# ScalarE takes the last six expert tiles and the last four weight sets; the closing sums move wholly to VectorE

## The chip, the core and the metric

The kernel runs on one core of one Trainium2 chip. Its engines work side by side, each through its own instruction queue: TensorE (PE, matmuls into PSUM), VectorE (DVE), ScalarE (ACT), GpSimd (POOL) and SyncE (SP, which here only issues DMAs). They meet through semaphores. The metric is the device time of one execution, in microseconds, lower is better; the figure shown is the median of three executions.

## The reference, cut to what matters

A small vision tower over 16 images of 256 tokens with 192 features: patch embedding at three scales, attention with 12 heads, and a mixture of 16 experts of which each token uses two. The experts are the part at stake:

```
logits = einsum('bld,ed->ble', x, Wr); probs = softmax(logits)
top_p, top_idx = top_k(probs, 2)                  # gate of token and expert
for each expert e:
    h   = gelu(x @ W1[e] + b1[e])                 # 192 -> 768
    out = h @ W2[e] + b2[e]                       # 768 -> 192
    y  += gate[e] * out
return x + y
```

So the output row of a token is its own row plus gate0 times the output of its first expert plus gate1 times that of its second. There are 16 x 256 x 2 = 8192 (token, expert) pairs.

## The kernel before

**Tiles.** The pairs are sorted by expert into tiles of 128 rows, each tile of one expert. What the router will choose isn't known when the program is built, so it always has the most tiles that can be needed: `NTILE` = 64 + 15 = 79. Tiles 0 to 14 (`NEARLY`) start while attention still runs; 15 to 78 are the stretch that fills the last 330 us. With the given inputs the sixteen experts get 310, 258, 1110, 987, 949, 269, 107, 460, 115, 555, 521, 471, 677, 449, 395 and 559 pairs; each rounded up to whole tiles makes 73. Tiles 0 to 72 hold rows, and 73 to 78 are padding: they are computed all the same, with rows that nobody asks for, and their results go to a part of `pair_rows` that isn't read.

**One tile.** GpSimd fetches its 128 rows from `slot_rows` in device memory into one of four buffers (`t_fetch`, L714). TensorE turns them (`t_rows`, L480, four transposes). VectorE works out where the results go and copies the turned rows out of PSUM (`t_across`, L656 to L661). TensorE multiplies by W1 (`t_up`, L494; both this and the next product run on halves of 64 rows, as two streams). ScalarE adds the bias and applies gelu (`t_gelu`, L530, six instructions). TensorE multiplies by W2 (`t_down`, L506); its two halves leave two partial sums in PSUM. VectorE adds the second bias and the two (`t_biased`, L669 and L670). GpSimd scatters the 128 rows into `pair_rows` (`t_place`, L704). TensorE's order is: up of tile t, turn of tile t+1, down of tile t-1.

**Weights.** SP loads them three tiles ahead into three buffers (`moe_loads`): for each tile two register loads that say which expert and whether it is a new one (L384, L385, `chosen`), two loads of halves of W1 (L392), the biases (L400) and W2 (L406). The loads have a condition: where the expert in the buffer is still the right one, nothing is moved and the semaphore counts on. Each waits until the buffer has been used: W1 of tile t until up of tile t-3, the biases until `m_y` says that the sum of tile t-3 is done, W2 until down of t-3.

**The closing sums.** When its last weight load is issued, SP reads four numbers into registers (L442), which are the counts of scatters that tiles with rows need. It waits for these scatters, not for those of the padding. Then it loads `pair_rows` back in order of tokens: eight chunks, each of two transfers of 384 KB, the first expert's rows into `pair[0]` and the second's into `pair[1]` (L448). ScalarE scales the second by its gate (L545, four instructions each chunk). VectorE multiplies the first by its gate and adds it to the token's row `hr` (L694, four instructions of 128x192), and then adds what ScalarE scaled (L700, one of 128x768). SP stores each chunk to `out` (L452). At the end SP waits for all stores and all 79 scatters.

The order on each engine is written out by hand. VectorE's and ScalarE's closing instructions come behind their last tile, SP's pair loads behind its last weight set.

Of the kernel before, what the change touches and what calls it, by code (L numbers as in the profile page):

```python
# [15 lines left out]
def vit_tower(nc, x0, x1, x2, w0t, w1t, w2t, b012, wft, bf, idx0, idx1, idx2, w_qkv, w_out, b_out, ln_g, ln_b,  # L16
              wrt, ew1, eb1, ew2, eb2, c_ident, c_tri, c_interp1, c_interp2, c_iota, out):
    fp32, bf16, i32, u32 = mybir.dt.float32, mybir.dt.bfloat16, mybir.dt.int32, mybir.dt.uint32
    ALU, ACT, AX = mybir.AluOpType, mybir.ActivationFunctionType, mybir.AxisListType
    ds = bass.ds  # L20

    P = 128
    B, T, E = out.shape
# [26 lines left out]
    NE, _, FF = ew1.shape  # L50
    FC = FF // P
    TOPK = 2
    PAIRS = TOPK * NT
    NTILE = PAIRS + NE - 1

    SEEN = 11
    NEARLY = 15
    assert TOPK * TT * SEEN - (NE - 1) >= NEARLY and NEARLY % 3 == 0
    NREST = NTILE - NEARLY
    NLANE, BY3, SHIFT = NREST // 4, 171, 9  # L60
    assert all(n * BY3 >> SHIFT == n // 3 for n in range(P))
    SEG = P + NT * P
# [22 lines left out]
    with ctx:  # L85
# [222 lines left out]
        def hidden(t):  # L308

            if t < NEARLY:  # L310
# [8 lines left out]
                 "pe_wT act_wT pe_wf act_wf dve_wf dve_g1 dve_b pe_x2T_ act_x2T_ pe_o2 dve_o2 st_o2 ld_x2 ld_o2 pe_x1T_ act_x1T_ pe_o1 act_o1 st_g2 st_g1 ld_g1 st_qA0 st_qA1 st_qB0 st_qB1 ld_qk0 ld_qk1 ld_mx0 ld_mx1 pool_var1 pool_var2 pool_var3 pool_ln pool_h2 pool_r "  # L319
                 "r_dve r_diagd pe_row pe_tot r_tab r_early "  # L320
                 "m_x0 m_x1 m_x2 m_x3 m_wa0 m_wa1 m_wa2 m_wb0 m_wb1 m_wb2 m_f0 m_f1 m_f2 m_f3 m_tr m_xT m_s1 m_gelu m_s2 m_y "
                 "m_sc0 m_sc1 m_sc2 m_sc3 ld_p0 ld_p1 ld_p2 ld_p3 ld_p4 ld_p5 ld_p6 ld_p7 c_first c_out c_gated "
                 "out_done dve_lane st_bias m_b0 m_b1 m_b2 r_hot").split()
        s = {n: sem(n) for n in names}

# [38 lines left out]
        def wait_prev(eng, which, count):  # L364

            if not (isinstance(count, int) and count <= 0):
                eng.wait_ge(which, count)


        def moe_loads(sp):  # L370
# [53 lines left out]
            second(1, *two)  # L424
            second(2, *three)
            before = None
            for t in range(NW, NTILE):
                if t == NEARLY:
                    biases(t - 1, *before)
                    second(t - 1, *before)  # L430
                    sp.wait_ge(s["r_tab"], 1)
                now = chosen(t)
                first(t, *now)
                if NW < t != NEARLY:
                    biases(t - 1, *before)
                    second(t - 1, *before)
                before = now
            biases(NTILE - 1, *before)
            second(NTILE - 1, *before)

            sp.wait_ge(s["r_hot"], 1)
            counts = [sp.value_load(r_tr[2][0:1, m:m + 1], min_val=16 * (PAIRS // NB), max_val=16 * (NTILE // NB + 1))  # L442
# [56 lines left out]
        def t_down(pe, t):  # L499
            p, w = t % 2, t % NW  # L500
            pe.wait_ge(s["m_gelu"], 2 if t == 0 else t + 1)
            pe.wait_ge(s[f"m_wb{w}"], 16 * (t // NW) + 16)
            wait_prev(pe, s["m_y"], t)
            for c in range(FC):
                for h, rows in enumerate((LO, HI)):
                    last = nc.tensor.matmul(Y[h], hT[p][rows, c * P:(c + 1) * P], w2b[w][rows, c, :],  # L506
                                            start=(c == 0), stop=(c == FC - 1))
            last.then_inc(s["m_s2"], 1)
# [14 lines left out]
        def t_gelu(act, t):  # L523
            p = t % 2
            w = t % NW
            act.wait_ge(s[f"m_b{w}"], 16 * (t // NW) + 16)
            act.wait_ge(s["m_s1"], t + 1)
            wait_prev(act, s["m_s2"], t - 1)
            for c in range(FC):
                last = nc.scalar.activation(hT[p][:, c * P:(c + 1) * P], hidden(t)[c], ACT.Gelu, bias=bias[w][:, c:c + 1])  # L530
            last.then_inc(s["m_gelu"], 1)

        def moe_scalar(act):
            for t in range(NEARLY, NTILE):
                t_gelu(act, t)
                if t == NEARLY + NREST // 2:
                    act.wait_ge(s["dve_ls"], B)
                    own = ex[:, NT - DEFER * TT:NT, :]
                    nc.scalar.activation(own, own, ACT.Exp).then_inc(s["act_ex"], 1)
                    nc.scalar.activation(warm[:, :], epsc[:, 0:1], ACT.Gelu)  # L540
            act.wait_ge(s["r_hot"], 2)
            for c in range(NC):
                act.wait_ge(s[f"ld_p{c}"], 32)
                for t in range(CT):
                    last = nc.scalar.activation(pair[1][c][:, t, :], pair[1][c][:, t, :], ACT.Copy,  # L545
                                                scale=r_gate[1][:, c * CT + t:c * CT + t + 1])
                last.then_inc(s["c_gated"], 1)

        done = [0]

# [120 lines left out]

        def moe_vector(dve):
            V = nc.vector
            for t in range(NEARLY - 2, NTILE):
                t_biased(dve, t)
                if t + 3 < NTILE:
                    t_across(dve, t + 3)
                if t == NEARLY + 4:
                    then(dve, V.tensor_scalar(r_tr[0][:, :], iota[:, 0:NB], ends[:, NE - 1:NE], float(NEARLY), ALU.add, ALU.add))
                    then(dve, V.tensor_scalar(r_tr[1][:, :], r_tr[0][:, :], 2, None, ALU.arith_shift_right))  # L680
                    then(dve, V.tensor_copy(r_trf[:, :], r_tr[1][:, :]))
                    V.tensor_scalar(r_tr[2][:, :], r_trf[:, :], 16.0, None, ALU.mult).then_inc(s["r_hot"], 1)
                if t == NEARLY + NREST // 2 + 2:
                    dve.wait_ge(s["act_ex"], B - DEFER + 1)
                    then(dve, V.tensor_reduce(r_sum[:, :], ex[:, :, 0:NE], AX.X, ALU.add))
                if t == NEARLY + NREST // 2 + 3:
                    then(dve, V.reciprocal(r_gate[0], r_sum[:, :]))
                    V.tensor_tensor(r_gate[1], ex[:, :, NE + 1], r_gate[0], ALU.mult).then_inc(s["r_hot"], 1)

            dve.wait_ge(s["pool_r"], B)  # L690
            for c in range(NC):
                dve.wait_ge(s[f"ld_p{c}"], 32)
                for t in range(c * CT, (c + 1) * CT):
                    last = V.scalar_tensor_tensor(hr[:, t, :], pair[0][c][:, t - c * CT, :], r_gate[0][:, t:t + 1],  # L694
                                                  hr[:, t, :], ALU.mult, ALU.add)
                last.then_inc(s["c_first"], 1)
                h = hr[:, c * CT:(c + 1) * CT, :]
                dve.wait_ge(s["c_gated"], c + 1)
                dve.wait_ge(s["c_first"], c + 1)
                V.tensor_tensor(h, h, pair[1][c], ALU.add).then_inc(s["c_out"], 1)  # L700

        def t_place(pool, t):
            pool.wait_ge(s["m_y"], t + 1)
# [1343 lines left out]
```

## Time and profile before

| | us |
|---|---|
| three executions | 808.65, 810.04, 814.27 |
| median | 810.04 |
| profiled execution, first to last instruction (span) | 776.9 |
| TensorE busy in it | 693.9 (89%) |
| VectorE busy | 459.1 (59%) |
| ScalarE busy | 372.5 (48%) |
| GpSimd busy | 389.3 (50%) |
| DMA queue of SP, share of 16 engines | 39.6% |

The own device time of the profiled execution isn't listed beside its span. The median of the three timed executions lies 33.1 us above that span (starting and ending the program). Busy shares are means over the whole span; what matters here is its last 50 us, which the rows below show.

In rows of a timeline or a chain the first number is the start in us from the beginning of the span, the second the time in us that the piece took. What stands in brackets behind a row is how long the engine had been idle and what ended that.

### The profile page before, as it was taken

What the parts mean: (1) busy time and instruction counts of PE and PEld (TensorE: products, weight loads), DVE (VectorE), ACT (ScalarE), POOL (GpSimd) and SP (SyncE); (2) the same over time, 40 slices, a digit from 0 to 9 for tenths busy, and PEclk for the clock granted to TensorE, in tenths of its full rate; (3) what the DMA queues carried; (4) which work ended last, traced back from release to release, by engine and by line L of the source; (5) the groups of instructions that cost most, each with busy time, mean ns of one, the idle gap of its engine ahead of it and who ended that gap; (6) DMA issues with size and microseconds to landing.
All of it is one profiled execution on the core that took longest, in us unless ns stands there. A gap on an engine that the chain in (4) does not pass through costs nothing.

```text
span 776.9 us, 22765 instructions
## 1 busy us (share of the span) xinstructions
PE 693.9 (89%) x7879; PEld 598.0 (77%) x7879; DVE 459.1 (59%) x1322; ACT 372.5 (48%) x892; POOL 389.3 (50%) x599
## 2 busy tenths in 40 slices
PE   0597689999999999999889999999999999999970
PEld 0486557777677777777657999999999999999970
DVE  7301345788888888888876764444444444443448
ACT  0232246666666666666565433334434453443443
POOL 6772123557777777777666553333433343343320
PEclk9999769999999999999999999999999999999995
DMA  8776624434444444444429634748348325498159
GB/s 208 140 114 190 140 60 108 112 89 121 103 110 103 111 115 114 109 109 111 108 66 264 189 106 121 220 141 227 91 128 236 97 76 149 123 288 240 50 182 331
DMA packets 96795, 110.69 MB, mean 142 GB/s; under 512 B 18625, under 2 KB 85186, under 8 KB 96386
## 3 DMA queue, kind: packets, MB, share of 16 engines
q1 hardware_dynamic: 79202, 79.56, 39.6%
q0 software_dynamic: 11792, 27.18, 11.7%
q10 hardware_dynamic: 5712, 2.79, 2.0%
q8 instruction: 52, 0.85, 0.5%
q14 instruction: 37, 0.30, 0.1%
HBM read 142.13 MB, written 33.96 MB: 227 GB/s over the span
## 4 chain that ended last, share of the span: by engine, by line
PE 57%; DVE 12%; issue 9%; POOL 8%; DMA 5%; SPq 4%; ACT 1%; POOLq 1%; DVEq 0%; ACTq 0%
PE BK L506 20%; PE BK L494 20%; PE BK L828 4%; PE BK L962 3%; PE BK L921 2%; POOL slot_rows L1896 2%; POOL rs L1845 2%; PE BK L941 2%; DVE negmax L1567 2%; DMA level_patches<-pixels 2%; POOL hr L1885 1%; DVE hr L694 1%; PE BK L973 1%; DMA level_rows<-shared 1%; SPq L746 1%
## 5 line engine op out<-in xcount | busy, mean ns | idle before, releaser
L530 ACT ACTIVATE pixels<-BK,shared 128x128 f32<-128x128 f32 x474 | 130.7, 375 | 197.1 <-PE BK L494 166.0
L494 PE MATMUL BK<-pixels,shared 64*128 64x128 f32 x2844 | 172.8, 272 | 2.0 <-issue 2.0
L506 PE MATMUL BK<-shared,pixels 64*128 64x192 f32 x1896 | 172.4, 328 | 2.3 <-DVE pixels L670 2.2
L704 POOL DMA_INDIRECT pair_rows<-pixels x79 | 77.9, 985 | 190.4 <-DVE pixels L670 183.9
L494 PEld LDWEIGHTS BK<-pixels,shared 64*128 64x128 f32 x2844 | 169.1, 188 | 3.3 <-issue 3.1
L506 PEld LDWEIGHTS BK<-shared,pixels 64*128 64x128 f32 x1896 | 153.3, 188 | 4.3 <-issue 3.9
L1567 DVE TENSOR_REDUCE negmax<-BK 128x6 f32<-128x1536 f32 x64 | 112.4, 1757 | 27.9 <-PE BK L941 26.6
L1317 ACT ACTIVATE shared<-BK 128x1536 f32<-128x1536 f32 x64 | 92.7, 1448 | 9.5 <-PE BK L962 9.1
L1896 POOL DMA_INDIRECT slot_rows<-xr,adr x64 | 64.7, 1011 | 36.8 <-issue 13.8
L669 DVE TENSOR_TENSOR pixels<-BK,shared 128x192 f32<-128x192 f32 x79 | 28.2, 357 | 71.1 <-PE BK L506 70.8
L656 DVE TENSOR_TENSOR pixels<-pixels 128x1 int32<-128x1 f32 x64 | 10.2, 159 | 89.9 <-PE BK L480 89.9
L941 PE MATMUL BK<-shared 96*128 96x256 bf16 x384 | 56.0, 284 | 4.5 <-DMA shared<-qk_parts 4.0
L962 PE MATMUL BK<-shared 99*128 99x256 bf16 x384 | 54.0, 278 | 0.7 <-ACT shared L1317 0.6
L1851 POOL TENSOR_TENSOR shared<-shared 128x512 bf16<-128x512 f32 (+1 forms) x32 | 29.1, 909 | 49.6 <-ACT shared L1298 48.9
L973 PE MATMUL BK<-shared,v 128*32 128x256 f32 x768 | 51.2, 385 | 1.0 <-ACT oT L1323 1.0
L941 PEld LDWEIGHTS BK<-shared 96*128 96x128 bf16 x384 | 36.0, 101 | 16.5 <-DMA shared<-qk_parts 4.4
L962 PEld LDWEIGHTS BK<-shared 99*128 99x128 bf16 x384 | 35.8, 99 | 12.3 <-ACT shared L1317 3.9
L714 POOL DMA_DIRECT2D pixels<-slot_rows x64 | 37.0, 578 | 4.2 <-issue 4.1
L1829 POOL DMA_INDIRECT pixels<-x,i x32 | 33.4, 1043 | 9.7 <-issue 9.7
L1323 ACT ACTIVATE oT<-BK 128x256 f32<-128x256 f32 x48 | 18.3, 381 | 39.0 <-PE BK L973 38.9
L1845 POOL TENSOR_TENSOR rs<-var,mhalf 128x2 f32<-128x2 f32 x48 | 34.0, 709 | 3.8
L973 PEld LDWEIGHTS BK<-shared,v 128*32 128x32 f32 x768 | 20.2, 109 | 17.3 <-issue 3.4
(239 smaller groups left out, 1073.6 us busy)
## 6 DMA issues: line engine op xcount, KB each, us to landing
shared<-ew SPq DMA_DIRECT2D x158, 288.0 KB
shared<-ew SPq DMA_DIRECT2D x79, 576.0 KB
shared<-qk_parts SPq DMA_DIRECT2D x112, 96.0 KB
shared<-expert_biases SPq DMA_DIRECT2D x79, 99.0 KB
pixels<-slot_rows POOLq DMA_DIRECT2D x64, 104.0 KB
qk_parts<-shared SPq DMA_DIRECT2D x32, 192.0 KB, 2.0
shared<-qk_parts SPq DMA_DIRECT2D x16, 288.0 KB
shared<-pair_rows SPq DMA_DIRECT2D x12, 384.0 KB, 7.6
```

What stands on the lines that cost most here:

```text
L494: last = nc.tensor.matmul(hidden(t)[h * HC + c], w1h[w][rows, (k + h) % NK, c * P:(c + 1) * P], xtT[p][rows, k, :], start=(c == 0 and k == ...
L506: last = nc.tensor.matmul(Y[h], hT[p][rows, c * P:(c + 1) * P], w2b[w][rows, c, :], start=(c == 0), stop=(c == FC - 1))
L530: last = nc.scalar.activation(hT[p][:, c * P:(c + 1) * P], hidden(t)[c], ACT.Gelu, bias=bias[w][:, c:c + 1])
L704: nc.gpsimd.indirect_dma_start(pair_d, bass.IndirectOffsetOnAxis(t_dst[:, t:t + 1], 0), ysum[t % NB][:, :], None).then_inc(s[f"m_sc{t % NB ...
L714: nc.gpsimd.dma_start(xt[t % NB][:, :], slot_d[ds(at, P), :]).then_inc(s[f"m_f{t % NB}"], 16)
L941: last = nc.tensor.matmul(S[:, a, t * T:(t + 1) * T], qs[p][0:KS, h, t * P:(t + 1) * P], ks[p][0:KS, h, :], start=True, stop=True)
L962: last = nc.tensor.matmul(dst[:, a, t * T:(t + 1) * T], ks[p][:, h, t * P:(t + 1) * P], qs[p][:, h, :], start=True, stop=True)
L973: last = nc.tensor.matmul(dst[32 * a:32 * a + 32, 0:T], v[p][:, t, GU * g + a, :], pT[:, GU * g + a, t * T:(t + 1) * T], start=(t == 0), s ...
L1317: nc.scalar.activation(pT[:, HU * u:HU * u + HU, :], src[:, :, :], ACT.Exp).then_inc(s["act_exp"], 1)
L1567: nc.vector.tensor_reduce(negmax[:, :, HU * u:HU * u + HU].rearrange("p t h -> p h t"), S[:, :, :].rearrange("p a (t k) -> p a t k", t=TT) ...
L1845: nc.gpsimd.tensor_tensor(rs[:, :], var[:, :], mhalf[:, :], ALU.pow).then_inc(done, 1)
L1896: nc.gpsimd.indirect_dma_start(slot_d, bass.IndirectOffsetOnAxis(adr[p][:, k, t:t + 1], 0), xr[p][:, t, k, :], None).then_inc(s[f"st_id{p} ...
```

## The change

`LATE` is 79 - 6 = 73 and `AHEAD` is 2.

- **SP** issues weight sets up to tile 74 instead of 78. Its register loads, waits and pair loads follow directly.
- **ScalarE** issues the weight sets of tiles 75 to 78 (`late_weights`), with the same register loads, waits and conditions. It also turns over the rows of tiles 75 to 78 (`late_across`: four instructions in place of VectorE's four) and copies the result of tiles 73 to 78 out of PSUM (`late_copied`). It no longer scales anything in the closing sums.
- **TensorE**: in tiles 73 to 78 down isn't split in halves: one matmul of the identity with the replicated second bias starts the sum, and six of 128 rows follow, all into one PSUM area, so that only a copy is left to do.
- **VectorE** stops after the sum of tile 72 and the turned rows of tile 74. Its closing sums have four instructions with the first gate and four with the second for each chunk.

```diff
+    LATE = NTILE - 3 * NE // 8
+    AHEAD = 2
 ...
-            for t in range(NW, NTILE):
+            for t in range(NW, LATE + AHEAD):
 ...
-            biases(NTILE - 1, *before)
-            second(NTILE - 1, *before)
+            biases(LATE + AHEAD - 1, *before)
+            second(LATE + AHEAD - 1, *before)
 ...
         # t_down
+            if t >= LATE:
+                nc.tensor.matmul(Y[0], ident[:, :], bias[w][:, FC:FC + E], start=True, stop=False)
+                for c in range(FC):
+                    last = nc.tensor.matmul(Y[0], hT[p][:, c * P:(c + 1) * P], w2b[w][:, c, :],
+                                            start=False, stop=(c == FC - 1))
+                last.then_inc(s["m_s2"], 1)
+                return
 ...
+        def late_across(act, t):
+            p = t % 2
+            act.wait_ge(s["m_tr"], t + 1)
+            nc.scalar.activation(t_dst[:, t:t + 1], xt[t % NB][:, E:E + 1], ACT.Identity, bias=offm[:, t:t + 1])
+            act.wait_ge(s["m_s1"], t - 1)
+            nc.scalar.activation(xtT[p][:, 0:2, :]..., XT[:, :, :, :]..., ACT.Copy)
+            nc.scalar.activation(xtT[p][LO, 2, :]..., XT[HI, :, 1, :], ACT.Copy)
+            nc.scalar.activation(xtT[p][HI, 2, :]..., XT[LO, :, 0, :], ACT.Copy).then_inc(s["m_xT"], 1)
+
+        def late_copied(act, t):
+            r = t % NB
+            act.wait_ge(s["m_s2"], t + 1)
+            act.wait_ge(s[f"m_sc{r}"], 16 * (t // NB))
+            nc.scalar.activation(ysum[r][:, :], Y[0], ACT.Copy).then_inc(s["m_y"], 1)
+
+        def late_weights(act, t):
+            w = t % NW
+            e = act.value_load(tab[0:1, t:t + 1], min_val=0, max_val=NE - 1)
+            new = act.value_load(r_new[0:1, t:t + 1], min_val=0, max_val=1)
+            act.wait_ge(s["m_s1"], t - NW + 1)
+            for h in range(2):
+                nc.scalar.dma_start(w1h[w][h * RT:(h + 1) * RT, :, :], ew1[...], cond=new) \
+                    .then_inc(s[f"m_wa{w}"], 16)
+            act.wait_ge(s["m_y"], t - NW + 1)
+            nc.scalar.dma_start(bias[w][:, :], bias_d[...], cond=new).then_inc(s[f"m_b{w}"], 16)
+            act.wait_ge(s["m_s2"], t - NW + 1)
+            nc.scalar.dma_start(w2b[w][:, :, :], ew2[...], cond=new).then_inc(s[f"m_wb{w}"], 16)
+
         def moe_scalar(act):
             for t in range(NEARLY, NTILE):
+                if t + 1 >= LATE + AHEAD and t + 1 < NTILE:
+                    late_across(act, t + 1)
                 t_gelu(act, t)
+                if t > LATE:
+                    late_copied(act, t - 1)
+                if LATE <= t < NTILE - AHEAD:
+                    late_weights(act, t + AHEAD)
 ...
-            act.wait_ge(s["r_hot"], 2)
-            for c in range(NC):
-                act.wait_ge(s[f"ld_p{c}"], 32)
-                for t in range(CT):
-                    last = nc.scalar.activation(pair[1][c][:, t, :], pair[1][c][:, t, :], ACT.Copy,
-                                                scale=r_gate[1][:, c * CT + t:c * CT + t + 1])
-                last.then_inc(s["c_gated"], 1)
+            late_copied(act, NTILE - 1)
 ...
         # moe_vector
-            for t in range(NEARLY - 2, NTILE):
+            for t in range(NEARLY - 2, LATE):
                 t_biased(dve, t)
-                if t + 3 < NTILE:
+                if t + 3 < LATE + AHEAD:
                     t_across(dve, t + 3)
 ...
             for c in range(NC):
                 dve.wait_ge(s[f"ld_p{c}"], 32)
-                for t in range(c * CT, (c + 1) * CT):
+                at = range(c * CT, (c + 1) * CT)
+                for t in at:
                     last = V.scalar_tensor_tensor(hr[:, t, :], pair[0][c][:, t - c * CT, :], r_gate[0][:, t:t + 1],
                                                   hr[:, t, :], ALU.mult, ALU.add)
                 last.then_inc(s["c_first"], 1)
-                h = hr[:, c * CT:(c + 1) * CT, :]
-                dve.wait_ge(s["c_gated"], c + 1)
                 dve.wait_ge(s["c_first"], c + 1)
-                V.tensor_tensor(h, h, pair[1][c], ALU.add).then_inc(s["c_out"], 1)
+                for t in at:
+                    last = V.scalar_tensor_tensor(hr[:, t, :], pair[1][c][:, t - c * CT, :], r_gate[1][:, t:t + 1],
+                                                  hr[:, t, :], ALU.mult, ALU.add)
+                last.then_inc(s["c_out"], 1)
```

How the instructions stand now is seen at two places. First VectorE at its last tile and its first closing chunk. `pixels` is the memory of the tiles' buffers, `BK` is PSUM, `shared` holds weights and the loaded pairs. Before (the last two sums, of tiles 77 and 78, have nothing between them):

```order
L661 COPY pixels<-BK 64x128
L669 TENSOR_TENSOR pixels<-BK,shared 128x192
L670 TENSOR_TENSOR pixels<-BK,pixels 128x192
L694 SCALAR_TENSOR_TENSOR hr<-shared,r_gates,hr 128x192 x4
L700 TENSOR_TENSOR hr<-hr,shared 128x768
```

and with the change, where the sum of tile 72 is the last:

```order
L705 COPY pixels<-BK 64x128
L713 TENSOR_TENSOR pixels<-BK,shared 128x192
L714 TENSOR_TENSOR pixels<-BK,pixels 128x192
L740 SCALAR_TENSOR_TENSOR hr<-shared,r_gates,hr 128x192 x4
L745 SCALAR_TENSOR_TENSOR hr<-shared,r_gates,hr 128x192 x4
```

The sums of tiles 73 to 78 and the copies of tiles 75 to 78 have left VectorE, and a chunk is eight instructions of 128x192 instead of four and one of 128x768.

Second ScalarE. Before, its last tiles are six gelu instructions each and nothing between them, then the scaling of the first chunks:

```order
L530 ACTIVATE pixels<-BK,shared 128x128 x186
L545 ACTIVATE shared<-shared,r_gates 128x192 x16
L545 ACTIVATE v<-v,r_gates 128x192 x8
L545 ACTIVATE xr<-xr,r_gates 128x192 x8
```

and with the change one of its tiles (75), from the turned rows of tile 76 to the weight set of tile 77:

```order
L545 ACTIVATE pixels<-pixels 128x1
L547 ACTIVATE pixels<-BK 128x256
L549 ACTIVATE pixels<-BK 64x128
L550 ACTIVATE pixels<-BK 64x128
L539 ACTIVATE pixels<-BK,shared 128x128 x6
L557 ACTIVATE pixels<-BK 128x192
L561 TENSOR_LOAD pixels
L562 TENSOR_LOAD pixels
L565 DMA shared<-ew 64x3x384
L570 DMA shared<-expert_biases 128x198
L573 DMA shared<-ew 128x6x192
```

Between two gelus of ScalarE now stand five more instructions, two register loads (with the register operations behind each, left out here as the second of the two W1 halves is) and four DMA issues.

## Rows read from the trace of the kernel before

**Rows 1.** The page's part 4: the chain that ended last, by engine

```profile
PE 57%; DVE 12%; issue 9%; POOL 8%; DMA 5%; SPq 4%; ACT 1%; POOLq 1%; DVEq 0%; ACTq 0%
```

**Rows 2.** By stretch: PE, PEld, DVE, ACT, POOL busy us, granted clock, DMA share, GB/s

```profile
720.00:730.00 10.00, 10.00 (x154) 10.00 (x152) 4.64 (x16) 4.97 (x18) 3.74 (x6) 1.00 0.19 59
```

**Rows 3.** The chain that ended last, in order of time: start, us, what

```profile
754.72 1.42 DVE hr L694 x4
...
756.23 0.96 DVE hr L700
757.19 1.33 DVE hr L694 x4
...
772.88 0.96 DVE hr L700
```

**Rows 4.** Timeline around tile 72: start, us, engine, line, operation

```profile
727.47 0.08 SPq L406 DMA_DIRECT2D shared<-ew  x1
...
730.80 0.36 DVE L670 TENSOR_TENSOR pixels<-BK,pixels 128x192 f32<-128x192 f32 x1
...
731.44 0.99 POOL L704 DMA_INDIRECT pair_rows<-pixels  x1 [2.31 <-DVE pixels L670]
...
732.47 1.66 ACT L530 ACTIVATE pixels<-BK,shared 128x128 f32<-128x128 f32 x6 [2.48 <-PE BK L494]
```

**Rows 5.** Timeline: SP's last weight loads, its first pair loads, its stores

```profile
737.26 0.54 SPq L392 DMA_DIRECT2D shared<-ew  x2
...
743.98 0.07 SPq L406 DMA_DIRECT2D shared<-ew  x1
...
746.63 4.28 SPq L448 DMA_DIRECT2D shared<-pair_rows  x9
...
757.21 17.03 SPq L452 DMA_DIRECT2D out<-hr  x8
```

**Rows 6.** Timeline: ScalarE as chunks 1, 2 and 8 land; GpSimd's last scatter

```profile
750.95 1.49 ACT L545 ACTIVATE shared<-shared,r_gates 128x192 f32<-128x192 f32 x4 [0.30 <-DMA shared<-pair_rows]
...
754.08 1.49 ACT L545 ACTIVATE shared<-shared,r_gates 128x192 f32<-128x192 f32 x4 [1.64 <-DMA shared<-pair_rows]
...
755.08 0.96 POOL L704 DMA_INDIRECT pair_rows<-pixels  x1 [2.19 <-DVE pixels L670]
...
766.74 1.49 ACT L545 ACTIVATE xr<-xr,r_gates 128x192 f32<-128x192 f32 x4 [0.45 <-DMA xr<-pair_rows]
```

**Rows 7.** DMA view 731.5 to 735.5, GB/s in 40 slices of 0.1 us

```profile
GB/s 0 0 0 0 0 0 0 0 0 0 0 0 0 0 0 553 184 154 93 0 0 0 291 455 166 175 50 25 0 0 0 0 0 0 0 0 42 0 0 0
```

**Rows 8.** DMA view 730 to 746: all packets, GpSimd's queue, SP's conditional W2 loads

```profile
DMA packets 279, 0.60 MB, mean 37 GB/s; under 512 B 96, under 2 KB 160, under 8 KB 276
...
q0 software_dynamic: 276, 0.56, 10.6%
...
shared<-ew SPq DMA_DIRECT2D x4, 576.0 KB
```

**Rows 9.** DMA view 774 to 777, the last store alone, 40 slices of 0.075 us

```profile
GB/s 0 0 0 0 0 0 0 0 0 0 113 297 348 328 297 328 328 328 328 328 328 328 317 328 328 328 226 41 0 0 0 0 0 0 0 0 0 0 0 0
DMA packets 528, 0.39 MB, mean 131 GB/s; under 512 B 16, under 2 KB 528, under 8 KB 528
```

**Rows 10.** DMA view 760 to 761, packets of GpSimd's queue

```profile
q0 software_dynamic: 8, 0.01, 3.3%
```

**Rows 11.** SP's pair loads, from issue to landing

```profile
DMA to landing us min/median/max: 3.3/8.9/12.2
```

**Rows 12.** TensorE by shape: down's halves, and full-row products (busy, mean ns)

```profile
L506 PE MATMUL BK<-shared,pixels 64*128 64x192 f32 x1896 | 172.4, 328 | 2.3 <-DVE pixels L670 2.2
...
L893 PE MATMUL BK<-lng_b,ident 128*128 128x192 f32 x56 | 11.8, 356 | 2.8 <-DMA pixels<-level_rows 2.8
...
L873 PE MATMUL BK<-w2f,shared 128*128 128x192 f32 x24 | 4.2, 330 | 0.0
```

**Rows 13.** ScalarE by line: a PSUM copy of 128x256

```profile
L1323 ACT ACTIVATE oT<-BK 128x256 f32<-128x256 f32 x48 | 18.3, 381 | 39.0 <-PE BK L973 38.9
```

More of the change, by code:

```diff
@@ L321, in vit_tower @@
                  "m_x0 m_x1 m_x2 m_x3 m_wa0 m_wa1 m_wa2 m_wb0 m_wb1 m_wb2 m_f0 m_f1 m_f2 m_f3 m_tr m_xT m_s1 m_gelu m_s2 m_y "
-                 "m_sc0 m_sc1 m_sc2 m_sc3 ld_p0 ld_p1 ld_p2 ld_p3 ld_p4 ld_p5 ld_p6 ld_p7 c_first c_out c_gated "
+                 "m_sc0 m_sc1 m_sc2 m_sc3 ld_p0 ld_p1 ld_p2 ld_p3 ld_p4 ld_p5 ld_p6 ld_p7 c_first c_out "
                  "out_done dve_lane st_bias m_b0 m_b1 m_b2 r_hot").split()
@@ L531, in t_gelu @@
             last.then_inc(s["m_gelu"], 1)
+        def late_across(act, t):
[3 more added lines that the diff above has]
+            act.wait_ge(s["m_s1"], t - 1)
+            nc.scalar.activation(xtT[p][:, 0:2, :].rearrange("p s (h t) -> p s h t", h=2),
+                                 XT[:, :, :, :].rearrange("p h s t -> p s h t"), ACT.Copy)
+            nc.scalar.activation(xtT[p][LO, 2, :].rearrange("p (h t) -> p h t", h=2), XT[HI, :, 1, :], ACT.Copy)
+            nc.scalar.activation(xtT[p][HI, 2, :].rearrange("p (h t) -> p h t", h=2), XT[LO, :, 0, :], ACT.Copy) \
+                .then_inc(s["m_xT"], 1)
@@ new lines, in late_copied @@
+        def late_copied(act, t):
[9 more added lines that the diff above has]
+            for h in range(2):
+                nc.scalar.dma_start(w1h[w][h * RT:(h + 1) * RT, :, :],
+                                    ew1[ds(e, 1), :, h * (FF // 2):(h + 1) * (FF // 2)].rearrange("a (k r) f -> r (a k) f", r=RT),
+                                    cond=new) \
+                    .then_inc(s[f"m_wa{w}"], 16)
+            act.wait_ge(s["m_y"], t - NW + 1)
+            nc.scalar.dma_start(bias[w][:, :], bias_d[ds(e, 1), :, :].rearrange("a p n -> p (a n)"), cond=new) \
+                .then_inc(s[f"m_b{w}"], 16)
+            act.wait_ge(s["m_s2"], t - NW + 1)
+            nc.scalar.dma_start(w2b[w][:, :, :], ew2[ds(e, 1), :, :].rearrange("a (c p) d -> p (a c) d", p=P),
+                                cond=new) \
+                .then_inc(s[f"m_wb{w}"], 16)
@@ L690, in moe_vector @@
             dve.wait_ge(s["pool_r"], B)
+            dve.wait_ge(s["r_hot"], 2)
             for c in range(NC):
                 dve.wait_ge(s[f"ld_p{c}"], 32)
-                for t in range(c * CT, (c + 1) * CT):
+                at = range(c * CT, (c + 1) * CT)
+                for t in at:
                     last = V.scalar_tensor_tensor(hr[:, t, :], pair[0][c][:, t - c * CT, :], r_gate[0][:, t:t + 1],
```

## The prediction

> **What bounds the kernel now.** I looked first at where the chain of waits ends. Over the whole span it is TensorE's, 57% [rows 1]; by stretches TensorE is busy all of 720 to 730 at full clock [rows 2], and only its own work can shorten that. The change touches nothing of it before tile 73. So the question is the tail. There the chain goes over to VectorE, to the closing sums, and stays on it to the end: the first chunk starts at 754.72 and the last instruction ends at 772.88 + 0.96 = 773.84 [rows 3]. The span ends at 776.9, 3.06 later: one store (its last packets pass at 774 + 28 x 0.075 = 776.1) and its semaphore [rows 9].
>
> A tile takes 1.66 + 2.48 = 4.14 us (ScalarE's work and its idle time between two gelus) [rows 4]. The sum of tile 72 ends at 731.16, its scatter is issued at 731.44 [rows 4]. SP's first pair load is issued at 746.63 [rows 5], 15 us later, though tile 72 is the last with rows. What held SP is its queue: the last weight load is issued at 743.98, and behind it are only four register loads, (746.63 - 744.05) / 4 = 0.65 us each [rows 5]. No time is left there for a wait on scatters. VectorE was held too: chunk 1 is in memory at 750.95 [rows 6], and its sum starts at 754.72, behind tile 78.
>
> **The change, part by part.**
>
> *SP is let go earlier.* Its last weight load, of tile 74, is issued at 727.47 [rows 4]; the register loads end at 727.55 + 2.58 = 730.1. Now a real wait comes last: tile 72's scatter. Its data pass from 733.0, the burst ending at about 733.4 (the second burst is GpSimd's fetch) [rows 7]. For the semaphore I add 0.6, between 0 and the 0.8 by which the last store's packets precede the end of the span [rows 9]. Pair loads from 734.0 (733.4 to 734.4), 12.6 earlier than 746.63.
>
> *The chunks land* as they did, counted from the first load: chunk 1 after 4.3, chunk 2 after 7.45, chunk 8 after 20.1 (ScalarE's starts in [rows 6] minus 746.63, where it had been idle for DMA): at 738.3, 741.45 and 754.1. Stores don't delay them in either kernel, since SP issues all sixteen loads first.
>
> *VectorE's chunk grows.* Before it is 1.33 + 0.09 + 0.96 = 2.38 (757.19 to 759.57) [rows 3]. The 0.96 becomes four instructions, 1.42 from a standing start [rows 3], so a chunk is 1.33 + 0.09 + 1.42 = 2.84. Chunk 1 ends at 741.2, before chunk 2 is there; from then on VectorE is the slower side: 741.45 + 7 x 2.84 = 761.3. That is 8 x 0.46 = 3.7 us of the gain given back, and ScalarE's scaling (1.49 per chunk [rows 6]) was no cost before, being hidden. With the last store 761.3 + 3.1 = **764.4**.
>
> *The stores as a floor.* They follow the loads in SP's queue. A lone one takes 17 slices of 0.075, 1.3 us [rows 9]; eight behind 754.1 make 764.5, and with the 0.8 behind the last packets 765.3 as an upper value, less where several are under way.
>
> *ScalarE's late tiles.* Before, it rests 2.48 of 4.14 us per tile [rows 4]. Added are: turned rows, one of 128x256 out of PSUM 0.38 [rows 13], two of 64x128 and one of 128x1 at no more than a gelu instruction each (1.66 / 6 = 0.28), 1.2 in all; the result 0.4 (between 1.49 / 4 and the 0.44 that a lone one may take) [rows 6]; a weight set, two register loads 1.3, the W1 pair 0.54, W2 0.07 [rows 5], biases with their register work about 0.4, together 2.3 to 2.4. Tiles 74, 75 and 76 cost 1.66 + 1.2 + 0.4 + 2.4 = 5.7 us, more than TensorE's period: ScalarE sets the pace there. Followed step by step from gelu 73 (up 73 ends near 728.2, as gelu 73 used to start at 728.3): ScalarE is free at 729.8, at 732.2 with weight set 75, at 738.1 with set 76, at 743.8 with set 77, at 749.5 with set 78. So up 77 starts at 745.1 and up 78 at 750.8, about 1 us of stall each, up 78 some 4 later than before. The last result is copied at 758.3, where VectorE's last ended at 754.4 before.
>
> *TensorE's unsplit down.* 24 half instructions become 14 full ones (each matmul of 32-bit data shows as two). Full-row products of the same width took 4.2 / 24 = 0.175 and 11.8 / 56 = 0.21 each [rows 12]: 2.45 to 2.95 per tile, against 172.4 / 79 = 2.18 [rows 12]. I take 2.5, as the cheaper row has the same kind of operands; partly hidden by ScalarE, the dearer end adds 1.0, 759.3.
>
> *The last scatter.* Issued 0.3 behind the result. With SP's queue full, a scatter issued at 755.08 still had packets between 760 and 761 [rows 6, 10], 5.9 later; in the quiet stretch it took 2.0 (731.44 to 733.4). So it ends between 758.6 + 2.0 and 759.6 + 5.9, plus 0.8: 761.4 to 766.3, beside the other ends and not behind them. SP waits for it last.
>
> *Conditional loads on ScalarE's queue.* Set t + 2 is now issued after gelu t: set 76 at about 737.5, needed at 739.4. In 730 to 746, where SP issues four whole sets that move nothing, there are 279 packets, 276 of them GpSimd's, and 0.60 MB [rows 8]. A transfer that moves data leaves 16 packets under 512 B beside its data (528 with them) [rows 9]; a skipped one leaves none. So I take its completion as 0 to 2 us, which costs nothing to 0.2. The Trainium skill (DMA: Bandwidth & Descriptors, Why a DMA increments its semaphore by 16 and not by 1) has the completion as each engine's last descriptor, a write that lands only after that engine's data. By it a skipped load would stand in line with the pair loads; that is rival 3.
>
> *Nothing else*: the row fetch of tile 78 is issued before the pair loads, no table load is added, and the tiles ahead of 73 are unchanged.
>
> **Sum.** Three ends stand at 764.4, up to 765.3, and 761.4 to 766.3. I take **765**: 776.9 - 765 = 11.9 us less. The profiled execution is known by its span alone; the median of 810.04 lies 33.1 above it, and I let that stand: 765 + 33.1 = **798**. Less than 1% (8.1 us, 801.9 to 818.1) can't be told from no change.
>
> **The rivals.**
>
> 1. *ScalarE and TensorE become the bound.* If a weight set costs 3 on ScalarE, full-row products 2.95 and each stall another 0.3, the last result comes 3 to 4 later, near 762, and with 0.3 + 5.9 + 0.8 the span ends at 769: 802. For it: ScalarE has no rest in three tiles. Against: only four sets move.
>
> 2. *VectorE and GpSimd block each other.* A sum now runs beside six scatters instead of one. If VectorE stood still for each (0.96 us), 6 x 0.96 = 5.8 us: 770, 803. The trace speaks against it: the sums from 754.72 take 1.42 beside the scatter of 755.08 [rows 3, 6], no more than elsewhere (1.33 on the chain behind others). The Trainium skill (SBUF — State Buffer, SBUF: two separate sides) says that a VectorE instruction with two SBUF inputs and a GpSimd instruction that reads SBUF take one port pair in turn, each for its whole length; by that the same price.
>
> 3. *Slower: skipped loads land like loaded ones.* If the semaphores of sets 76 to 78 come L after the issue, tile 76's up waits, and set 78, issued later for it, makes tile 78's wait again, so beyond about 3 us each us of L costs 2. With L = 8.9, the median of pair loads [rows 11], the last result is at 770.4, the span ends near 774, 807. With 12.2, their longest [rows 11], at 777.0, plus 0.3 + 2.0 + 0.8 = 780.1: 813, slower than before. It decides from L = 10.6, where 773.8 + 3.1 = 776.9. Against: the missing packets [rows 8].
>
> 4. *It doesn't do what it says.* If SP's counts included padding, its wait would move to tile 78's scatter, and 30.3 us (746.63 to 776.9) would follow 761: 791, 824. But SP started its loads at 746.63, before tile 76 was scattered, and without any wait.
>
> **How the numbers follow.** Forecast 0.62; rival 1, 0.17; rival 2, 0.05; rival 3, 0.07; rival 4, 0.02; below 794 (chunks landing sooner in a quiet queue) 0.03; something unseen, slower, 0.04. The range: 761.4 + 33.1 = 794 is the low end (all ends at their early values, and no tail behind VectorE's 761.3); up to 805 it takes in rivals 1 and 2; left out are rivals 3 and 4 and the unseen, about 0.16. Faster by over 1%: the forecast, the early case and three quarters of rival 1, 0.78. Within 1%: the rest of rival 1, rival 2, most of rival 3, 0.17. Slower: 0.05.
>
> **What would show it.** Right: SP's first pair load near 734; VectorE's first closing instruction near 738, its last ending near 761, eight chunks 2.84 apart without DMA waits after the second; idle time of TensorE of about 1 us ahead of up 77 and up 78; ScalarE's last copy near 758 and the last scatter near 765. Wrong: ScalarE's late period above 6 us, up 76 waiting for weights (rival 3), sums above 0.35 us apart while scatters are issued (rival 2), or a first pair load after 740 (rival 4).

## The result: 795.85 us, and the profile after

| | before | after |
|---|---|---|
| median of the runs, us | 809.35 (808.18 to 814.27, 4 runs) | 795.85 (794.4 to 801.02, 4 runs) |
| ratio, 95% interval | | 0.9843 (0.98 to 0.9886) |
| span of the profiled execution | 776.9 | 795.1 |
| from the end of tile 72's sum to the end of the span | 45.7 | 33.1 |

The kernel is 13.5 us faster, by the ratio 9 to 16 us. The forecast was 798. That the span of the trace after is longer than that of the first trace of before, with a shorter device time, is taken up below: the first trace lacks a stretch of idle time at the start which every later trace but one (pads_first) has. So the two are compared from the end of tile 72's sum on: 731.16 before (730.80 + 0.36) [rows 4], 761.96 after. From here on "+x" is x us behind that sum.

The timeline after, around tile 72 and the first chunks (start, us, engine, line, operation; in brackets the idle time ahead of it and what ended it):

```profile
761.60 0.36 DVE L714 TENSOR_TENSOR pixels<-BK,pixels 128x192 f32<-128x192 f32 x1
...
762.24 0.99 POOL L751 DMA_INDIRECT pair_rows<-pixels  x1 [2.31 <-DVE pixels L714]
...
764.99 5.74 SPq L450 DMA_DIRECT2D shared<-pair_rows  x9
...
769.84 1.40 DVE L740 SCALAR_TENSOR_TENSOR hr<-shared,r_gates,hr 128x192 f32<-128x192 f32 x4 [7.88 <-DMA shared<-pair_rows]
...
771.27 1.41 DVE L745 SCALAR_TENSOR_TENSOR hr<-shared,r_gates,hr 128x192 f32<-128x192 f32 x4
...
772.66 1.40 DVE L740 SCALAR_TENSOR_TENSOR hr<-shared,r_gates,hr 128x192 f32<-128x192 f32 x4
```

SP's first pair load is at +3.03, where it was at +15.5 [rows 5], and VectorE's first closing sum at +7.9, where it was at +23.6 (754.72) [rows 3]. VectorE has one wait left, for the first chunk. SP's longest is for a scatter; its other long ones, of up to 3.5 us, are between the stores, for VectorE's sums. The waits of SP after, from 760 on (who waited for whom, us in total, times, longest):

```profile
SPq L454 <- DVE hr L745: 9.7, 6, 3.5
SPq L447 <- DMA pair_rows<-pixels: 4.1, 1, 4.1
SPq L87 <- DMA out<-hr: 1.9, 1, 1.9
```

L447 is the wait for the scatters of tiles with rows; before it did not show, as its engine came to it late. The chain of what waited last (start, us, what) now runs over that scatter and the first chunk's load, to VectorE's sum at 769.84:

```profile
762.24 2.67 DMA pair_rows<-pixels
...
765.39 4.31 DMA shared<-pair_rows
```

L458, at the very end, is the wait for the scatters of all 79 tiles, and the 1.9 us of L87 behind it are the wait for the last store. The end of the chain after (start, us, what) answers to [rows 3]:

```profile
785.14 1.41 DVE hr L745 x4
786.55 1.33 DVE hr L740 x4
...
787.90 1.41 DVE hr L745 x4
789.31 1.33 DVE hr L740 x4
...
790.66 0.42 DVE hr L745
791.08 0.33 DVEq L87
791.41 0.66 DVE hr L745 x2
```

A chunk is 1.41 + 1.35 = 2.76 (785.14 to 787.90; the 1.35 is the 1.33 and 0.02 before the next), without waits, and VectorE ends at 791.41 + 0.66 = 792.07, +30.1; the span ends 3.03 later.

ScalarE and TensorE after, from up 76 to up 77: the copy of tile 74's result, weight set 77, down 75, gelu 76; and the last copy and the last scatter:

```profile
770.49 2.28 PE L496 MATMUL BK<-pixels,shared 64*128 64x128 f32 x36
...
771.10 0.37 ACT L557 ACTIVATE pixels<-BK 128x192 f32<-128x192 f32 x1
...
771.95 0.53 ACTq L565 DMA_DIRECT2D shared<-ew  x2
...
772.82 0.59 PE L507 MATMUL BK<-shared,ident 128*128 128x192 f32 x2
...
773.25 2.11 PE L509 MATMUL BK<-shared,pixels 128*128 128x192 f32 x12
...
774.43 1.67 ACT L539 ACTIVATE pixels<-BK,shared 128x128 f32<-128x128 f32 x6
...
775.29 2.28 PE L496 MATMUL BK<-pixels,shared 64*128 64x128 f32 x36
...
787.90 0.33 ACT L557 ACTIVATE pixels<-BK 128x192 f32<-128x192 f32 x1 [2.69 <-PE BK L509]
788.51 0.97 POOL L751 DMA_INDIRECT pair_rows<-pixels  x1 [2.06 <-ACT pixels L557]
```

The late period (from one tile's first product to the next one's) is 775.29 - 770.49 = 4.80, and TensorE fills it. Before the change it was 4.13 (742.57 to 746.70). The unsplit down accounts for 2.54 - 2.20 = 0.34 of the difference if its length alone is counted; no run asked where the rest comes from. The last result is copied at 788.23, +26.3.

### The profile page after: what moved, and what is told of

It reads as the page before. It is cut to its first block, busy times and chain, and to the rows that moved or that the text cites. A ratio compares the mean times of both kernels' runs of the same rounds, so it can differ in the third digit from the quotient of the medians.

```text
span 795.1 us, 22622 instructions
## 1 busy us (share of the span) xinstructions
PE 699.7 (88%) x7819; PEld 601.2 (76%) x7819; DVE 454.0 (57%) x1318; ACT 367.9 (46%) x882; POOL 387.7 (49%) x599
## 4 chain that ended last, share of the span: by engine, by line
issue 38%; PE 18%; POOL 16%; DVE 13%; another core or an unknown queue 5%; POOLq 4%; DMA 3%; ACT 2%; SPq 1%; DVEq 0%; ACTq 0%
POOL pixels L761 5%; PE BK L875 4%; POOL slot_rows L1943 3%; PE BK L1009 3%; POOLq L760 3%; PE BK L968 2%; POOL pair_rows L751 2%; POOL rs L1892 2%; DVE negmax L1614 2%; PE BK L988 2%; PE BK L1020 2%; POOL hr L1932 2%; DVE hr L745 1%; DVE hr L740 1%
## 5 line engine op out<-in xcount | busy, mean ns | idle before, releaser
L496 PE MATMUL BK<-pixels,shared 64*128 64x128 f32 x2844 | 175.1, 273 | 1.8 <-issue 1.7
L515 PE MATMUL BK<-shared,pixels 64*128 64x192 f32 x1752 | 160.0, 328 | 3.0 <-DVE pixels L714 1.6
L515 PEld LDWEIGHTS BK<-shared,pixels 64*128 64x128 f32 x1752 | 142.3, 187 | 4.7 <-issue 3.9
L713 DVE TENSOR_TENSOR pixels<-BK,shared 128x192 f32<-128x192 f32 x73 | 26.1, 357 | 42.8 <-PE BK L515 39.8
L1890 POOL TENSOR_TENSOR var<-mv,epsc 128x2 f32<-128x2 f32 x48 | 9.3, 194 | 73.3 <-DVE mv L1579 73.2
L1370 ACT ACTIVATE oT<-BK 128x256 f32<-128x256 f32 x48 | 18.4, 383 | 40.5 <-PE BK L1020 40.5
L1892 POOL TENSOR_TENSOR rs<-var,mhalf 128x2 f32<-128x2 f32 x48 | 34.1, 710 | 3.8
L1876 POOL DMA_INDIRECT pixels<-x,i x32 | 30.7, 961 | 9.7 <-issue 9.7
```

Source lines behind the costliest of these rows:

```text
L496: last = nc.tensor.matmul(hidden(t)[h * HC + c], w1h[w][rows, (k + h) % NK, c * P:(c + 1) * P], xtT[p][rows, k, :], start=(c == 0 and k == ...
L1892: nc.gpsimd.tensor_tensor(rs[:, :], var[:, :], mhalf[:, :], ALU.pow).then_inc(done, 1)
```

## The experiments

All times are ratios to runs of the kernel before on the same chip. The tail is read from each trace as above, from the end of tile 72's sum to the end of the span; it is not touched by what varies earlier (that sum ends anywhere between 760 and 766 in the traces). Each tail is one trace's.

| run | ratio, 95% interval | first pair load | first sum | tail |
|---|---|---|---|---|
| before, second trace | 0.9993 (0.9959 to 1.0027) | +15.5 | +23.55 | 45.8 |
| SP alone let go | 1.0006 (0.9978 to 1.0033) | +2.7 | +23.56 | 45.8 |
| VectorE alone let go | 1.0026 (1.0001 to 1.0051) | +17.35 | +21.8 | 47.1 |
| both gates on VectorE, nothing else | 1.0058 (1.0023 to 1.0093) | +15.5 | +23.56 | 48.8 |
| change, scaling left on ScalarE | 1.0026 (1.0002 to 1.005) | +3.3 | +7.9 | 48.3 |
| change, late W2 products twice | 0.9957 (0.9933 to 0.9981) | +3.2 | +8.0 | 42.0 |
| change, ScalarE scales three chunks | 0.9821 (0.9788 to 0.9855) | +2.9 | +8.2 | 33.2 |
| change, second trace | 0.9804 (0.9767 to 0.9842) | +2.9 | +8.7 | 33.9 |

**The kernel before again (base_again).** No edit.

> The kernel before, unchanged, for a second trace. Theory A: the 33.1 us that I put outside the span of the first trace are a stretch inside, at the start (the changed kernel's trace has TensorE, VectorE and ScalarE idle from about 34 to 64 us, and only 1.7 us outside its span). Then the span is about 807, 1.7 below the device time, with that idle stretch in it, and from the sum of tile 72 to the end it is 45.7 us as in the first trace. Rival: the idle stretch came with the change; then the span is about 777 and has no such stretch. Time 809, ratio 1.00 by both.

Span 811.4 with a tail of 45.8 (about 807 was expected; that execution took 813.71). The stretch is there. By stretch (PE, PEld, DVE, ACT, POOL busy us, clock, DMA share, GB/s), first in the first trace of before, then in this one:

```profile
40.00:60.00 20.00, 18.25 (x127) 15.66 (x125) 0.56 (x1) 7.20 (x10) 15.43 (x18) 1.00 0.78 121
```

```profile
40.00:60.00 20.00, 0.00 (x0) 0.00 (x0) 0.00 (x0) 0.00 (x0) 13.70 (x16) 1.00 0.26 49
```

Its waits of 20 to 90 us:

```profile
ACT w2f L1252 <- remote: 39.5, 1, 39.5
PE BK L828 <- ACT b1T L1256: 31.9, 1, 31.9
DVE hbias L1510 <- remote: 26.7, 1, 26.7
```

From about 34 to 64 GpSimd is the only one of the four computing engines that works; SP issues loads until about 41. Theory A holds: outside the span lie 1.7 us (796.82 against 795.1 in the profiled execution after), and about 30 of the 33.1 that I put outside are this stretch. It was there in the changed kernel as well, so it cancels between the two. No execution of the kernel before on record came below 806.49, though its first trace spans only 776.9: the first trace is the odd one. "Remote" says that the profile doesn't know who released the two engines.

**SP alone (sp_alone).** The kernel before, with `late_weights` in ScalarE's loop and SP's loop ending at tile 74:

```diff
-            for t in range(NW, NTILE):
+            for t in range(NW, LATE + AHEAD):
 ...
                 t_gelu(act, t)
+                if LATE <= t < NTILE - AHEAD:
+                    late_weights(act, t + AHEAD)
```

> The kernel before, with the last four weight sets issued by ScalarE, so that SP goes on to the pair loads; VectorE keeps all its tiles and ScalarE the scaling. Theory (both must be let go): pair loads start 3 us after the sum of tile 72 instead of 15.5, but VectorE begins its closing sums behind tile 78 as before, 23.5 us after the sum of tile 72; the tail from that sum to the end stays 45.7 us (45.3 to 46.5), time 809. Rival (SP's queue is what held the tail): 12.4 us less, 33 us, time 797.

The sum of tile 72 ends at 764.52 here. Pair loads at +2.7, VectorE's first sum at +23.56, tail 45.8:

```profile
767.24 5.67 SPq L450 DMA_DIRECT2D shared<-pair_rows  x9
...
788.08 1.41 DVE L716 SCALAR_TENSOR_TENSOR hr<-shared,r_gates,hr 128x192 f32<-128x192 f32 x4
```

12.8 us earlier loads bring nothing. The rival falls.

**VectorE alone (dve_alone).** The changed kernel, SP's loop to `NTILE` again, `late_weights` not called.

```diff
-            for t in range(NW, LATE + AHEAD):
+            for t in range(NW, NTILE):
 ...
-                if LATE <= t < NTILE - AHEAD:
-                    late_weights(act, t + AHEAD)
```

> The changed kernel, but SP issues all 79 weight sets as before; ScalarE has the late tiles, VectorE is free from tile 73 on and does both gates. Theory (both must be let go): SP's last set waits for the sum of tile 75, 14.4 us behind that of tile 72 at the slower late period of 4.8, so the first pair load comes at 17.5; plus 7.45 for chunk 2, 7 x 2.78 for the sums and 3.05 for the last store is a tail of 47.5 us, 1.8 more than before: 811. Rival (VectorE's release is what gives it): a tail near 33, 797.

VectorE stands idle for the first chunk:

```profile
788.13 1.41 DVE L738 SCALAR_TENSOR_TENSOR hr<-shared,r_gates,hr 128x192 f32<-128x192 f32 x4 [21.80 <-DMA shared<-pair_rows]
```

The tail is 47.1, 1.3 us longer than before (1.8 expected). Each half of the change alone is worth nothing or less, both together 12.6 us in the first trace's tail and 11.9 in the second's: whichever engine is still held sets the start of the sums.

**Both gates on VectorE (sums_alone).** The kernel before with the changed closing sums.

```diff
-                h = hr[:, c * CT:(c + 1) * CT, :]
-                dve.wait_ge(s["c_gated"], c + 1)
-                V.tensor_tensor(h, h, pair[1][c], ALU.add).then_inc(s["c_out"], 1)
+                for t in at:
+                    last = V.scalar_tensor_tensor(hr[:, t, :], pair[1][c][:, t - c * CT, :], r_gate[1][:, t:t + 1],
+                                                  hr[:, t, :], ALU.mult, ALU.add)
+                last.then_inc(s["c_out"], 1)
```

> The kernel before, but VectorE adds both gated halves of a chunk itself (eight instructions of 128x192) and ScalarE scales nothing. Theory: VectorE is the bound of the closing stretch from 23.5 us after the sum of tile 72 on, and a chunk costs 2.78 instead of 2.38, so 8 x 0.4 = 3.2 us more: tail 48.9, time 812.5. Rival (the wait for ScalarE was part of the chunk, or transfers bound it): no difference, 45.7 and 809.

Tail 48.8, 3.0 us more: this is what the change pays back, 8 x 0.38.

**The scaling left on ScalarE (scal_keeps).** The changed kernel with the old closing loop on both engines, ScalarE's behind its last copy.

```diff
             late_copied(act, NTILE - 1)
+            act.wait_ge(s["r_hot"], 2)
+            for c in range(NC):
+                act.wait_ge(s[f"ld_p{c}"], 32)
+                ... (four instructions with scale, c_gated)
```

> The changed kernel, but ScalarE scales the second half of each chunk as before the change, behind its last copy, and VectorE adds 128x768. Theory (the scaling had to leave ScalarE, since its queue now ends 26.3 us behind the sum of tile 72): chunk 1 can be finished only at 27.8, then 2.38 each, tail 27.8 + 0.96 + 7 x 2.38 + 3.06 = 48.5 us against 33.1, time near 811 to 813. Rival (a chunk of 2.38 instead of 2.76 wins, ScalarE is idle enough): tail 30 to 33, time at or below the changed kernel.

VectorE starts at +7.9 and then waits 18.4 us for ScalarE (its one wait for L596, the scaling); tail 48.3 (48.5 expected). Left behind ScalarE's last tile, the scaling costs the whole gain and more. Where ScalarE has no weight set left to issue there is room for some of it, as scal_helps below shows.

**The late products twice (down_twice).** In padding tiles the W2 products are added a second time, into rows that nobody reads.

```diff
-                for c in range(FC):
+                for c in range(2 * FC):
+                    c, end = c % FC, c == 2 * FC - 1
```

> The changed kernel, with the six W2 products of each padding tile done twice (their results are not read, the output is unchanged). It asks how far TensorE's late tiles are from the bound. A late period of 4.8 becomes 6.9, so the last copy moves from 26.3 to 38.9 us behind the sum of tile 72, and the last scatter with its wait follows some 3 to 6 later. Theory: TensorE's side takes over, tail 42 to 45 us against 33.1, time near 806; VectorE's sums end where they did, 30 us behind that sum. Rival (the end waits for the stores alone): 33.1.

Its late tiles take 6.75 (from copy to copy; 6.9 expected), and the last result is copied at +38.0 (38.9 expected). Its waits of SP:

```profile
SPq L458 <- DMA pair_rows<-pixels: 9.5, 1, 9.5
SPq L454 <- DVE hr L746: 8.2, 4, 3.3
SPq L447 <- DMA pair_rows<-pixels: 4.2, 1, 4.2
```

L458 is the last wait for scatters; it was 0.2 us in the changed kernel and is 9.5 here. VectorE's last sum ends at +30.7, half a microsecond later than it did. So the mechanism of rival 1 of the prediction is real, but it needs more: 11.7 us of added time on TensorE's side (last copy at +38.0 instead of +26.3) made the tail 8.9 longer. By this, TensorE's side had 2.8 us of slack. In the changed kernel itself SP came out of the wait for the last scatter 1.9 us before the last store landed, and that scatter's packets passed until 792.4, 3.9 us behind its issue at 788.51, beside stores; in down_twice, with the stores done, they took 2.3 (799.24 to 801.5). So the slack is 2 to 3 us, and part of it appears only because a later scatter passes sooner.

**ScalarE scales three chunks (scal_helps).** Chunks 5, 7 and 8, behind the results of tiles 76, 77 and 78, so that VectorE has 128x768 there.

```diff
+        SCALED = {77: (4,), 78: (6,), 79: (7,)}
 ...
+                for c in SCALED.get(t, ()):
+                    scaled(act, c)
```

> The changed kernel, but ScalarE scales chunks 5, 7 and 8 in gaps of its late tiles (behind the results of tiles 76, 77 and 78). Theory (VectorE's eight chunks are the bound from 7.9 us behind the sum of tile 72 to 3 us before the end): three chunks are 0.4 shorter, tail 31.9 to 32.2 instead of 33.1; the last scatter, whose packets end some 2 us before the last store's, is the next bound. Rival (stores or scatter bound it already): 33.1 again. Over the whole 0.1%, less than the timed runs can tell; the tail in the trace decides.

VectorE's eight chunks took 21.5 (772.23 to 793.70) instead of 22.2, though it also waited 0.55 for chunk 2. It began 0.35 us later than in the changed kernel, so its last sum is at +29.7, 0.4 earlier. The tail is 33.2 all the same, as the rival had it; the 31.9 to 32.2 of the theory did not come. SP's queue is full at 789 to 790 (first row: packets, MB, share of 16 engines) and still at 795 to 796 (second row):

```profile
q1 hardware_dynamic: 503, 0.37, 110.5%
```

```profile
q1 hardware_dynamic: 387, 0.28, 91.5%
```

In the changed kernel the traffic had run down to 20 to 30 GB/s from 792.4 to 792.9, before its last store. The span ends 3.5 us behind VectorE's last sum, where it was 3.03. So of the 0.75 us that VectorE's stretch became shorter, 0.35 went into the later start and 0.47 into stores still in line. With one trace this shows that VectorE and the stores end close to each other, and no gain that the timed runs could tell.

**The changed kernel again (after_again).** No edit.

> The changed kernel, unchanged, for a second trace and a narrower time. Theory: tail from the sum of tile 72 to the end 33.1 us (32.8 to 33.6), so 12.6 us less than before, time 0.984 to 0.985 of before; the idle stretch from 34 to 64 us is there as in the kernel before. Rival (part of the measured 13.5 us is chance in the start stage): the ratio is nearer to 0.99, with the same tail.

Tail 33.9, 11.9 us less than the second trace of before; 32.8 to 33.6 was expected. The 33.1 of the first trace was the short end. The three kernels below have the same closing stretch, and their tails are 34.1, 33.5 and 34.3. In all five traces the tail is 25.3 to 25.5 behind VectorE's first sum (+7.9, +8.7, +8.8, +8.2, +8.8), so what varies is when the first chunk lands.

The whole is 0.9804 (0.9767 to 0.9842), where 0.984 to 0.985 was expected: faster by 12.8 to 19 us. What it has beyond the tail, 0 to 7 us, no trace explains; the end of tile 72's sum differs by as much from trace to trace.

**The stall at the start (pads_first, pads_mid, pads_8th).** The changed kernel, with GpSimd's two stores of padding rows ahead of its 32 gathers, behind 16 of them, and behind 8.

```diff
+            pool.wait_ge(s["dve_init"], 4)
+            nc.gpsimd.dma_start(slot_d[0:NE * SEG, :]... (padt), and the same for padt2
             pool.wait_ge(s["ld_idx0"], 16)
             for c in range(TT):
                 for g in range(GP):
 ...
-            (the two stores, behind the gathers)
```

> The changed kernel, with GpSimd's two stores of padding rows (1.66 MB each) issued before its 32 gathers instead of behind them. All traces but the first of the kernel before have TensorE, VectorE and ScalarE idle from 34 to 64 us; they go on when the first of these stores has landed (its small last packets pass between 64 and 65). Theory: the stall hangs on GpSimd's queue and ends with the stores; with the stores at about 21 us it ends before 35 and 25 to 30 us go, time near 768. Rival 1: it hangs on the gathers; the engines go on near 61 to 65 as before, time 796 to 800. Rival 2: the stall has to do with neither; the same.

> The changed kernel, with GpSimd's two stores of padding rows issued behind 16 of its 32 gathers (at about 37 us instead of 56.6). In the run with the stores first VectorE went on at 34.1 without the stall, but SP's loads of the level-2 and level-1 rows stood behind the stores. Theory (the stall from 34 us on ends when the first store has landed): the engines go on at 43 to 47 instead of 64, 17 to 20 us less, time 777 to 782. Rival (the stall isn't tied to the stores, and their place only moves other waits): time 794 to 798.

> The same with the stores behind 8 of the 32 gathers, at about 27 us. Theory (the stall ends with the first store's landing): the stall ends at 33 to 37, but the row loads of SP, which run until 40, share the DMA engines with 3.3 MB of stores (some 10 us); time 770 to 785, and level with or below the run behind 16. Rival: 794 to 798.

With the stores first, VectorE goes on at 34.10 and ScalarE at 34.03, not at 64. But the row loads are late: VectorE then waits until 46.31 and TensorE until 50.26 for them,

```profile
50.26 5.21 PE L875 MATMUL BK<-ident,shared 128*128 128x128 f32 x44 [16.27 <-DMA shared<-level_patches]
```

and TensorE's next products come in pieces until 68. It is busy for 2.27 us of 60 to 65, and from 65 to 70 it is granted 0.50 of its clock, that is 1.2 of 2.4 GHz, where the changed kernel's traces have 1.00. The first product of attention comes at 91.60, against 96.80 and 98.64 in the two traces of the change: of 30 us of stall, 5 to 7 are gained by then. The ratio is 0.9781 (0.9748 to 0.9814), level with the change within the intervals, and far from the 768 us of the theory.

Behind 16 and behind 8 gathers the stall is as it was; ScalarE goes on at 63.90 and 63.29:

```profile
63.90 1.13 ACT L1299 ACTIVATE w2f<-BK 128x1152 f32<-128x1152 f32 x1 [39.20 <-remote]
```

```profile
63.29 1.13 ACT L1299 ACTIVATE w2f<-BK 128x1152 f32<-128x1152 f32 x1 [38.60 <-remote]
```

with ratios 0.9845 (0.9812 to 0.9877) and 0.9812 (0.9772 to 0.9851). My theory, that the stall ends when the first store lands, has fallen: the stores were issued up to 30 us earlier, their data had passed by 53 (behind 16) and 44 (behind 8), and the end of the stall moved by less than 1. Why it is absent with the stores ahead of all gathers, and in the first trace of before, the runs don't tell; what holds three engines from 34 to 64 us stays open. None of these versions beats the change by more than the intervals.

## Why the prediction was right

- **SP let go.** This is the heart of the mechanism, and it held. Forecast 2.84 behind the sum of tile 72 (734.0), measured 3.03; 12.4 us earlier for 12.6. The wait for the scatter is now real, 4.1 us of it.
- **Chunks landing.** 4.3 from the first load was too little. Chunk 1 came 4.85 later here and 5.8 in the second trace.
- **VectorE's chunk.** 2.76 instead of 2.84: the second group follows on the first almost without a gap, where I had kept the 0.09 of the wait before the large instruction. I also had VectorE wait for chunk 2; it did not wait again. The shorter chunks and the missing wait make up for the late first chunk, so the last sum ended at +30.1, as forecast (761.3 - 731.16). That they cancel to 0.1 us is luck: in the second trace the last sum is at +30.8.
- **Last store.** 3.03 for 3.06. The sum of these, 33.1 of tail, was forecast as 764.4 - 731.16 = 33.2; I had taken 33.8 for the three ends together. The second trace has 33.9.
- **ScalarE's late tiles.** This term was mis-sized. I took 5.7 us per tile, with 1.3 for two register loads; the period is 4.80 and TensorE sets it. The copy of tile 74's result ends at 771.47 and the first W1 issue starts at 771.95, only 0.48 behind it. At tile 73 it even starts before the gelu ahead of it has ended (759.52 + 1.66 = 761.18):

```profile
759.52 1.66 ACT L539 ACTIVATE pixels<-BK,shared 128x128 f32<-128x128 f32 x6 [2.49 <-PE BK L496]
...
761.05 0.62 ACTq L565 DMA_DIRECT2D shared<-ew  x2
```

  So the register loads of ScalarE's queue run beside the instructions ahead of them, and adding them in full to its work was the error. A weight set took 1.5 behind the copy (771.47 to 773.02, 776.32 to 777.82), where I had 2.3 to 2.4. With gelu 1.67, the turned rows 1.14 (773.26 to 774.40) and the copy 0.37 ScalarE's tile is 4.7: it does not set the pace, but it has hardly any rest left. The forecast stall of about 1 us each ahead of up 77 and up 78 did not come. The error cost nothing; the last copy came at +26.3 instead of +27.1.
- **TensorE's unsplit down.** 773.25 + 2.11 - 772.82 = 2.54, forecast 2.5.
- **The last scatter and the stores** were forecast as ends near VectorE's, and are. The scatter was in at about +30.7, near the early end of the forecast (+30.2 to +35.1) and before the +34 that I had named as the sign; down_twice finds 2 to 3 us of slack behind it. For the stores scal_helps finds half a microsecond at most.
- **Conditional loads.** Set 77 is issued at 771.95 and tile 77's up starts at 775.29 on time; nobody waited. Set 78 has 3.34 us (776.75 to 780.09), as little. Rival 3, that skipped loads stand in line with the pair loads, did not happen; no run measured the completion itself.
- **Rival 2.** Sums beside GpSimd's scatters take 1.40 to 1.41 for four as elsewhere; issuing a scatter went from 0.96 or 0.99 to at most 1.11 in this trace and 1.18 in the second (1.68 once in scal_helps). The Trainium skill (SBUF — State Buffer, SBUF: two separate sides) has the two take one port pair in turn, each for its whole length; the trace shows no such block on VectorE.
- **33.1 us outside the span** was wrong as a reading. I had a median and a span from different executions and took the difference for starting and ending the program. Since it sits in both kernels, the difference of the two was not touched, and the absolute time came out by that luck alone. A forecast in per cent of a stage at the start would have failed.

## What to carry to other kernels

When a closing stage waits behind another on two queues, look for all that holds it: here each release alone was worth nothing and both were worth about 12 us. Work that is left over for a kernel whose size is only known at run time (padding) is best put on engines whose queues hold nothing that must follow it. A move that costs 0.38 us per chunk on the bound engine can be right, if the cheaper place sits behind 20 us of other work; and after it look at which ends stand together before shortening the next one.

## What the runs showed of the hardware

- **A scatter beside a full queue.** The scatter issued at 755.08 had packets until 760 to 761 [rows 6, 10]; the quiet one of 731.44 was done in 2 us [rows 7]. The profile lists the two as queues of their own; the delay is there all the same. The Trainium skill (DMA: Bandwidth & Descriptors, Queues, rings and completion order) has a DMA engine take turns between queues, a whole packet at each turn; whether such turns add up to this delay no run here shows.
- **Two engines issuing DMAs at a time.** SP's first nine pair loads took 5.74 us to issue in the changed kernel, 5.67 in sp_alone and 6.42 in the second trace of the change, where ScalarE issues weight sets; in all traces where ScalarE issues them they took 5.30 to 6.64. In the traces where ScalarE issues none they took 4.28 [rows 5], 4.48, 4.61 (sums_alone) and 4.23. The last of these is dve_alone, the changed kernel but for that:

```profile
783.69 4.23 SPq L450 DMA_DIRECT2D shared<-pair_rows  x9
```

  The loads themselves and how many are issued are the same. The first chunk came 4.44 us behind the first load in dve_alone, 4.65 where the nine took 5.30 (scal_keeps), and 5.9 where they took 6.64 (pads_8th). That the late first chunk comes from this is likely and wasn't tried by itself.
- **Idle for 30 us with nothing named.** The stretch from 34 to 64 us is in all traces but the first one of before and the one with the stores first. It is more than twice as long as what this change gains. That its end would bring that much isn't shown: in pads_first the engines then waited for late row loads instead.
